# Recommender tower: the low weights' subtraction behind the gathers, the first embeddings in a quarter and a rest, and a shared relu in the first and last chunk

## What is computed

```python
e = stack([tbl_f[ids[:, f]] for f in range(39)], axis=1)   # 2048 x 39 x 16
x0 = xk = e
for W, b in layers:                                         # three layers of 128
    z = relu(einsum('bhd,bkd,hks->bsd', x0, xk, W) + b[None, :, None])
    xk, direct = z[:, :64], z[:, 64:]                       # last layer: all 128 direct
h = concat([sum_over_d(all direct parts), dense_ctx], axis=1)
y = relu(relu(h @ W_top1 + b_top1) @ W_top2 + b_top2) @ W_top3
```

## Time and profile before

| | us |
|---|---|
| median of 3 runs | 2478.97 (2478.65 to 2479.06) |
| time of the profiled execution | 2477.58 |
| its span, first to last instruction | 2475.8 |

### The profile page before, as it was taken

The page is one execution under the profiler, slowest core; times in us unless marked ns, Lnnn a source line. Parts: engine busy times, 40 slices in busy tenths (PEclk is TensorE's granted clock), DMA queues, the critical chain, the costliest instruction groups (busy, mean ns, idle before and its releaser), DMA issues.

```text
span 2475.8 us, 33269 instructions
## 1 busy us (share of the span) xinstructions
PE 2422.1 (98%) x8854; PEld 1640.9 (66%) x8854; DVE 2211.2 (89%) x1876; ACT 1724.4 (70%) x2185; POOL 1948.6 (79%) x1331
## 2 busy tenths in 40 slices
PE   5999999999999999999999999999999999999989
PEld 2566666666666666666666666666666666666655
DVE  1599999999989999999999999899999999999990
ACT  1677777777767777767777776676777777677663
POOL 6688888888878888888888888788888888865550
PEclk9899999999999999999999999999999999999999
DMA  3778667766856766776686677577668667766830
GB/s 74 157 145 175 141 138 160 158 137 141 175 124 139 174 134 140 163 157 137 144 172 138 139 161 160 121 157 160 137 139 174 145 139 154 164 136 134 171 84 0
DMA packets 214716, 352.60 MB, mean 142 GB/s; under 512 B 34382, under 2 KB 47566, under 8 KB 214588
## 3 DMA queue, kind: packets, MB, share of 16 engines
q1 hardware_dynamic: 194717, 347.07, 65.4%
q0 software_dynamic: 19968, 5.15, 2.1%
HBM read 346.97 MB, written 5.12 MB: 142 GB/s over the span
## 4 chain that ended last, share of the span: by engine, by line
PE 54%; POOL 26%; issue 14%; DVE 4%; ACT 1%; POOLq 0%; DMA 0%; ACTq 0%; DVEq 0%
PE ps L858 20%; POOL Pl L397 11%; POOL emb L391 11%; PE ps L868 11%; PE ps L848 10%; PE ps L836 8%; PE ps L831 2%; POOL dir L426 2%; DVE P L731 1%; DVE ps L731 1%; DVE Pl L736 1%; PE ps L983 1%; POOL sqx L403 1%; PE ps L975 1%; PE ps L824 1%
## 5 line engine op out<-in xcount | busy, mean ns | idle before, releaser
L397 POOL TENSOR_TENSOR Pl<-P,Ph 128x1024 fp32r<-128x1024 f32 x448 | 1074.8, 2399 | 285.3 <-ACT Ph L541 261.5
L858 PE MATMUL ps<-Ph,wh 128*128 128x512 f32 x2048 | 965.2, 471 | 9.9 <-ACT Ph L541 9.9
L541 ACT ACTIVATE Ph<-ps 128x1024 fp32r<-128x1024 f32 x576 | 590.3, 1025 | 406.7 <-DVE ps L731 393.0
L731 DVE TENSOR_TENSOR P<-xb,ps 128x1024 f32<-128x1024 f32 x704 | 853.2, 1212 | 2.8 <-DMA xb<-x_dram 2.8
L736 DVE TENSOR_TENSOR Pl<-ps,Ph 128x1024 fp32r<-128x1024 f32 x576 | 705.1, 1224 | 116.1 <-ACT Ph L541 97.4
L858 PE MATMUL ps<-Ph,wl 128*128 128x512 f32 x1920 | 755.5, 393 | 0.0
L868 PE MATMUL ps<-Pl,wh 128*128 128x512 f32 x2048 | 742.2, 443 | 7.4 <-POOL Pl L397 7.4
L391 POOL DMA_INDIRECT emb<-tbl_in,idx x624 | 600.6, 962 | 170.5 <-issue 145.0
L731 DVE TENSOR_TENSOR ps<-xb,ps 128x1024 f32<-128x1024 f32 x576 | 707.1, 1228 | 28.5 <-issue 9.4
L541 ACT ACTIVATE Ph<-P 128x1024 fp32r<-128x1024 f32 x448 | 473.9, 1058 | 186.1 <-DVE P L731 129.8
L868 PEld LDWEIGHTS ps<-Pl,wh 128*128 128x128 f32 x2048 | 384.3, 188 | 200.0 <-issue 118.2
(11 more groups left out here) (68 smaller groups left out, 857.2 us busy)
## 6 DMA issues: line engine op xcount, KB each, us to landing
xb<-x_dram SPq DMA_DIRECT2D x1280, 256.0 KB
emb<-tbl_in,idx POOLq DMA_INDIRECT x624
x_dram<-rows SPq DMA_DIRECT2D x64, 78.0 KB
xb<-w_in SPq DMA_DIRECT2D x16, 128.0 KB
xb<-wt_in SPq DMA_DIRECT2D x2, 512.0 KB, 4.4
xb<-dense_in SPq DMA_DIRECT2D x1, 768.0 KB, 5.3
wp<-w_in SPq DMA_DIRECT2D x4, 128.0 KB
xb<-w0a_in SPq DMA_DIRECT2D x1, 448.0 KB
```

Of the source, the lines that this page charges most:

```text
L397: pool.tensor_tensor(Pl[:, h_slot(ref, c, k)], P[:, p_slot(ref, c, k)], Ph[:, h_slot(ref, c, k)], ALU.subtract).then_inc(low_pool, 1)
L541: act.activation(Ph[:, h_slot(ref, c, k)], p, ACT.Copy).then_inc(rounded, 1)
L731: dve.tensor_tensor(p, xb[:, x], xk.unsqueeze(1).broadcast_to([128, 2, N]), ALU.mult)\
L858: pe.matmul(z_of(c, k), w[:, q, j, :], Ph[:, h_slot(ref, c, k), j, :], start=k in (L1B, L2) and i + j == 0, stop=False)
```

## The change

1. DVE's subtraction for `wl` and the two copies after it move from the weight preparation to behind DVE's work on the first embeddings. PE and SP wait for five weight signals at the start; PE waits for all eight only before g = 1. The staged weights move to the end of `xb`, in slots that the first spreads don't touch.
2. The first tile's embeddings are prepared in two parts: columns 0 to 3 (`D0`) first, then columns 4 to 15 (`D1`). ACT does high and full for `D0` and high for `D1`; DVE does low for `D0`, low for `D1` and full for `D1`. PE's first transposes wait for the `D0` part alone.
3. For chunk 0 ACT copies `x2` before `rows`, and PE's first two sums wait for `x2` alone.
4. In chunk 0 (first layer) and in the last chunk (second layer) DVE does the relu of the lower half in place while ACT does the direct part; ACT then copies the lower half to the upper half.
5. POOL issues 11 gathers instead of 14 ahead of the low part of k = 7, and 7 instead of 4 behind it. `WARM` is 37 instead of 36.

```diff
--- before.py
+++ after.py
@@ -34,7 +34,7 @@
 
 
 PRE = 4
-WARM = 36
+WARM = 37
 L1B, L2, STEPS = PAIRS - PRE, PAIRS, 2 * PAIRS
 KIND = "GVPVGPVGVPVGVGVGVGVP"
 SPL = [k for k in range(STEPS) if KIND[k] != "P"]
@@ -59,6 +59,7 @@
 SINGLE_STEPS = [k for k in range(STEPS) if TURN[k % PAIRS] == SINGLE // 2]
 assert all(k in SPL for k in SINGLE_STEPS)
 CHUNKS = TILES * CPT
+D0, D1 = slice(0, DC), slice(DC, D)
 NEXT_IDS_AT = (2, 0)
 GATHERS = [[1, 2, 3, 5, 9, 14, 16, 18, 19], [1, 2, 3, 5, 6, 8, 9, 10],
            [1, 2, 3, 5, 6, 9, 10, 12, 14, 16, 18, 19], [1, 2, 3, 5, 6, 8, 9, 10, 18, 19]]
@@ -185,6 +186,9 @@
         sel = sel0[0:R2, 0:T0 * R0].rearrange("p (t r) -> p t r", r=R0)
         sel0_st, inc = stage(R2, T0, R0), stage(R0, T0, NF)
         w0a_st, w0b_st = stage(R0, T0, S), stage(R0, T0, S)
+        assert at[0] + NS * 2 * S <= XSLOTS * 2 * N
+        at[0] = XSLOTS * 2 * N - NS * 2 * S
+        assert at[0] >= 2 * PRE * 2 * N
         w_st = stage(128, NS, 2 * S).rearrange("p q (j m) -> p q j m", j=2)
 
         xt = xb[:, :, :, :].rearrange("p q j n -> p (q j) n")
@@ -231,6 +235,10 @@
         emb_high = sem("emb_high")
         emb_low = sem("emb_low")
         emb_full = sem("emb_full")
+        first_high = sem("first_high")
+        first_full = sem("first_full")
+        first_low = sem("first_low")
+        first_x = sem("first_x")
         settled = sem("settled")
         aux_ready = sem("aux_ready")
         aux_read = sem("aux_read")
@@ -329,8 +337,8 @@
                         .then_inc(xb_in[q], 16)
 
 
-            sp.wait_ge(weights_made, 8)
-            sp.wait_ge(parts_made, 2)
+            sp.wait_ge(weights_made, 5)
+            sp.wait_ge(parts_made, 3)
             write_rows(0, 0)
             for p in range(PRE):
                 spread(0, p)
@@ -442,7 +450,7 @@
                 take_ids(T)
 
             next_ids(1)
-            early, early2 = 14, 18
+            early, early2 = 11, 18
             for f in range(early):
                 gather(f)
             for k in range(L1B, L2):
@@ -556,9 +564,18 @@
                 act.activation(dir1[:, COL1[c % CPT], :], z2_ps, ACT.Relu, bias=bias[:, 2:3]).then_inc(z2_read, 1)
 
 
-            high_emb(0)
-            full_emb(0)
-            copy_x(0, 0)
+            def part(x, d):
+                return x[:, :, d].rearrange("p f d -> p d f")
+
+            act.wait_ge(gathered, 16 * NF)
+            act.activation(emb_h[:, :, D0], emb[:, :, D0], ACT.Copy).then_inc(first_high, 1)
+            act.activation(emb2[:, D0, 0, :], part(emb, D0), ACT.Copy).then_inc(first_full, 1)
+            act.activation(emb_h[:, :, D1], emb[:, :, D1], ACT.Copy).then_inc(emb_high, 1)
+            act.wait_ge(aux_ready, 1)
+            act.activation(x2[:, :], aux_ps[0:R2], ACT.Copy).then_inc(first_x, 1)
+            act.activation(rows_sb, aux_ps[0:NF], ACT.Copy).then_inc(rows_ready, 1)
+            act.wait_ge(rows_ready, 1)
+            act.sem_inc(aux_read, 1)
             square(0, 2, 0, early_ps[0][1])
             rest_squares(0, 0, 1, early_ps[0][0])
             for t in range(1, FULL0):
@@ -566,9 +583,8 @@
             act.wait_ge(squares_done, 1)
             direct0(0)
             act.wait_ge(z0_read, 1)
-            upper(0, z0_ps[:, 0], xk1_upper)
             act.wait_ge(xk1_upper, 1)
-            lower(0, z0_ps[:, 0], xk1_ready)
+            act.activation(z0_ps[hi, 0], z0_ps[lo, 0], ACT.Copy).then_inc(xk1_ready, 1)
 
             act.wait_ge(rows_written, 16)
             copy_x(0, AUX)
@@ -632,9 +648,13 @@
                             direct1(c)
                         if k == RELU1_AT:
                             act.wait_ge(z1_read, T * CPT + c + 1)
-                            upper(1, z1_ps[:, c % 2], xk2_upper)
-                            act.wait_ge(xk2_upper, T * CPT + c + 1)
-                            lower(1, z1_ps[:, c % 2], xk2_ready)
+                            if end:
+                                act.wait_ge(xk2_upper, CHUNKS)
+                                act.activation(z1_ps[hi, c % 2], z1_ps[lo, c % 2], ACT.Copy).then_inc(xk2_ready, 1)
+                            else:
+                                upper(1, z1_ps[:, c % 2], xk2_upper)
+                                act.wait_ge(xk2_upper, T * CPT + c + 1)
+                                lower(1, z1_ps[:, c % 2], xk2_ready)
                         if KIND[k] != "P" and (CPT * ref + c, k) in STEPSET:
                             round_(T, ref, c, k)
                         if end and k == L1B:
@@ -698,17 +718,9 @@
             dve.wait_ge(weights_made, 1)
             dve.tensor_scalar(w0[:, :, :], w0a_st[:, 0:FULL0], 0.5, None, ALU.mult).then_inc(weights_made, 1)
             dve.tensor_scalar(w0b_st[:, FULL0], w0a_st[:, FULL0], 0.5, None, ALU.mult).then_inc(weights_made, 1)
-            dve.wait_ge(parts_made, 2)
-            dve.tensor_tensor(wl[:, :, :, :], w_st, wh[:, :, :, :], ALU.subtract).then_inc(weights_made, 1)
-
             dve.wait_ge(parts_made, 3)
             part = slice(GAP, GAP + REST)
             dve.tensor_tensor(w0x[part, :], w0b_st[part, FULL0], w0x[part, :], ALU.subtract).then_inc(weights_made, 1)
-
-            dve.wait_ge(weights_made, 5)
-            for k in SINGLE_STEPS:
-                q = SPL.index(k)
-                dve.tensor_copy(wh[K1:, q, 1, :], wl[K1:, q, 1, :]).then_inc(weights_made, 1)
 
             dve.wait_ge(incident, 1)
             dve.scalar_tensor_tensor(out=w0[0:NF, 0, :], in0=aux_ps[0:NF, 0:S], scalar=-0.5, in1=w0a_st[0:NF, 0, :],
@@ -742,9 +754,24 @@
                 dve.wait_ge(rest_square, chunk + 1)
                 dve.tensor_tensor(sqx[LOWS, :], rest_sq, sqx[LOWS, :], ALU.subtract).then_inc(rest_ready, 1)
 
+            def lower(layer, z, made):
+                dve.tensor_scalar(z, z, bias[lo, layer:layer + 1], 0.0, ALU.add, ALU.max).then_inc(made, 1)
+
+            def part(x, d):
+                return x[:, :, d].rearrange("p f d -> p d f")
+
+            dve.wait_ge(first_high, 1)
+            dve.tensor_tensor(emb2[:, D0, 1, :], part(emb, D0), part(emb_h, D0), ALU.subtract).then_inc(first_low, 1)
             dve.wait_ge(emb_high, 1)
-            dve.tensor_tensor(emb2[:, :, 1, :], emb[:, :, :].rearrange("p f d -> p d f"),
-                              emb_h[:, :, :].rearrange("p f d -> p d f"), ALU.subtract).then_inc(emb_low, 1)
+            dve.tensor_tensor(emb2[:, D1, 1, :], part(emb, D1), part(emb_h, D1), ALU.subtract).then_inc(emb_low, 1)
+            dve.tensor_copy(emb2[:, D1, 0, :], part(emb, D1)).then_inc(emb_full, 1)
+            dve.wait_ge(parts_made, 2)
+            dve.tensor_tensor(wl[:, :, :, :], w_st, wh[:, :, :, :], ALU.subtract).then_inc(weights_made, 1)
+            dve.wait_ge(weights_made, 6)
+            for k in SINGLE_STEPS:
+                q = SPL.index(k)
+                dve.tensor_copy(wh[K1:, q, 1, :], wl[K1:, q, 1, :]).then_inc(weights_made, 1)
+
             def low_weights():
                 dve.wait_ge(mlp_high, 1)
                 r = slice(2 * GAP, DX)
@@ -755,6 +782,8 @@
                         .then_inc(mlp_low, 1)
 
             rest_low(0)
+            dve.wait_ge(squares_done, 1)
+            lower(0, z0_ps[lo, 0], xk1_upper)
             dve.wait_ge(xk1_ready, 1)
             waiting = None
             for s in range(PRE):
@@ -779,6 +808,9 @@
                                 waiting = None
                             if k == L2 - 1:
                                 low_weights()
+                                dve.wait_ge(plain_done, PLAINS[CHUNKS - 1, L1B - 1])
+                                dve.wait_ge(split_done, SPLITS[CHUNKS - 1, L1B - 1])
+                                lower(1, z1_ps[lo, (CPT - 1) % 2], xk2_upper)
                             continue
                         if k == L1B:
                             dve.wait_ge(xk1_ready, T * CPT + c + 2)
@@ -897,16 +929,25 @@
                 pe.matmul(z1_ps[:, 0], wp[:, 0, 0, :], wp[:, 0:2].rearrange("p q j m -> p (q j m)"), start=True, stop=True)
 
 
-            pe.wait_ge(weights_made, 8)
+            pe.wait_ge(weights_made, 5)
             pe.wait_ge(parts_made, 1)
             pe.wait_ge(idx_ready, 2)
-            pe.wait_ge(emb_full, 1)
-            pe.wait_ge(emb_low, 1)
+            pe.wait_ge(first_full, 1)
+            pe.wait_ge(first_low, 1)
             late = None
             for g in range(2):
+                if g:
+                    pe.wait_ge(weights_made, 8)
+                    pe.wait_ge(emb_full, 1)
+                    pe.wait_ge(emb_low, 1)
                 transposes(g)
-                pe.wait_ge(aux_read, READS * g + 1)
+                if g:
+                    pe.wait_ge(aux_read, READS + 1)
+                else:
+                    pe.wait_ge(first_x, 1)
                 for i, t in enumerate((FULL0, 0, 1)):
+                    if i == 2 and not g:
+                        pe.wait_ge(aux_read, 1)
                     sums(t, early_ps[g][i])
```

## The result

The changed kernel took 2483.39 us (median of 12 runs, 2481.15 to 2485.74) beside 2479.32 us for the kernel before (12 runs): the ratio is 1.0018, with a 95% interval of 1.001 to 1.0026. It is 4 us slower, not 7 us faster. The profiled execution took 2484.04 us, its span is 2482.2.

The account below looks back on a forecast made before the run. PE, busy 98% of the span, was taken as the bound. Entering its unbroken work 6.65 us earlier plus 0.48 in the last chunk gave 7.1, so 2478.97 - 7.1 = 2471.9 us; range 2469.6 to 2475.2.

Parts of the forecast that it names:

- the first part of PE's side: Start: moving the `wl` subtraction frees a gather, 3.95 us saved; moved copies cost nothing, as PE is in warm-up matmuls.
- D: Rival, slower: clock stays at half through both groups until POOL's k = 0; 5.1 us slower, 2484.1; chance 0.04.
- The gather: POOL's early gather loses its wait for DVE's `wl` subtraction: 1.08 us instead of 5.03, saving 3.95.
- The quarter first: First embeddings: preparing a quarter first lets transposes follow the last gather after 0.84 us instead of 2.18, saving 1.34.
- `x2` first: Chunk 0: PE's first sums wait for one copy instead of two, saving 0.61 us.
- Relu: DVE's relu beside ACT's direct part: 0.71 us saved in chunk 0, 0.48 in the last chunk.
- POOL: Ids' copy held behind the moved `wl` subtraction; low part of k = 0 at 89.95 instead of 96.76, lead 6.8 us.
- The sum: PE's lead 6.6 and POOL's 6.8 let PE enter 6.65 us earlier; with the last chunk's 0.48, 7.1 us.
- The granted clock: Sign at PE in chunk 0: forecast is wrong if the clock is at half beyond 65 us or beyond 82.

Follow-up runs that it names:

- group 3: Changed kernel unchanged 2470.11 us beside 2477.86 for the kernel before, no slow stretch; with the subtraction moved back 2474.44; with 24 warm-up matmuls 2470.16.
- group 4: Changed kernel unchanged 2485.14 us, with the slow stretch; kernel before 2476.73; changed kernel with the subtraction moved back 2476.27; with 24 warm-up matmuls 2472.47.
- the first profile: Profile of the changed kernel, unchanged, from the result's own runs, with the slow stretch; that execution took 2484.04 us.
- group 2: Changed kernel unchanged 2483.65 us beside 2477.43 for the kernel before; with 36 warm-up matmuls 2482.92; with 60, 2502.1; all with the slow stretch.
- the run with the pause: Changed kernel with POOL clearing the unused buffer Pl ahead of the 14th gather: 2473.58 us, ratio 0.9988 to the kernel before.
- groups 1, 3 and 5: Changed kernel in 1: 24 warm-up matmuls 2470.79 us, 36 2470.64, subtraction back 2475.15; in 5: unchanged 2472.23, POOL pause 2473.58, early DVE work 2469.59; group 3 above.

## Why the prediction was wrong

**The step that failed** is in the first part of PE's side: that PE "is in its warm-up matmuls, whose end is 54.2 [...] and which the 37th moves to about 55.1, still before the first transposes below". I took the pace of those matmuls as given because nothing in the change touched them. They ended at 71.6 (at 55.4 in group 3, without the slow stretch), and the transposes, 14.3 us later than forecast, waited for nothing else. That this is the loss is shown by the changed kernel without the slow stretch (2470.11 in group 3) and by group 4, where 24 matmuls instead of 37 gave back 12.7 us on one chip. No rival had it: D was a loss on PE by the granted clock, which stood at its full level when the passes slowed down; that its 2484.1 lies next to the measured 2483.39 is luck. In the kernel before a delayed warm-up would have had 8.29 us of idle time in which to hide half of such a delay of 16; the change shortens that cover to about 2 us, so that what happens to unused work decides when the used work begins.

**What it costs.** The marks of the third layer in the profiles: 143.6 with the slow stretch against 132.3 in group 3's profile of the same kernel, 11.3 us, while the transposes differ by 71.47 - 57.82 = 13.7. The last 20 passes have brought the clock back, so that chunk 0's first layer runs at the full one, and at ACT's direct part the difference is 12.6 (82.31 and 69.68). At POOL's low part of k = 0 it is 11.6 (101.59 and 89.99): in group 3 that part comes 0.42 us behind POOL's own gathers, with the slow stretch POOL has long issued them and waits 2.91 us for ACT. The medians, 2483.4 and 2470.1, differ by 13.3; some 2 us of that lie in the loop, whose marks span 2274.4 us in the first profile, 2272.2 before, 2271.9 in group 3's and 2267.4 in group 2's (146.8 to 2414.2). I don't explain these.

**The other steps, by the profile of group 3 where nothing else is said.**
- The gather: 0.94 us instead of 5.03, and no wait under the small subtraction. Saved 4.1; forecast 3.95. An earlier one, at 18.6 us, took 1.83 (1.68 in the first profile) instead of 1.33. ACT's start in the first profile moved by 60.31 - 56.46 = 3.85. With the subtraction back the long gather is there again (5.02) and the kernel is slower by 4.3 us: that term is shown by removal.
- The quarter first: 56.86 to 57.82 is 0.96 us instead of 2.18, saved 1.22; forecast 1.34. DVE's piece took 0.43, not 0.34.
- `x2` first: PE's sums start 0.65 us after ACT (58.90 to 59.55) instead of 1.26, saved 0.61 as forecast.
- Relu, by the first profile: 0.63 in chunk 0 (82.31 to 83.76 instead of 75.66 to 77.74; forecast 0.71), 0.49 in the last (forecast 0.48). DVE's relu took 0.74 to 0.75, not 0.65, ACT's copy 0.57, not 0.62.
- POOL: the ids' copy was held to the end of the subtraction, 59.74 + 4.21 = 63.95, and k = 0 began at 89.99; forecast 89.95. With the subtraction back the copy took 0.21 to 0.22. The Trainium skill, SBUF — State Buffer, section "SBUF: two separate sides", has the lock last for the whole instruction, where a DVE instruction with two SBUF inputs takes it only against a GpSimd instruction that reads SBUF; the copy agrees. So does its other side: in the run with the pause, POOL's clear of a buffer reads nothing, and DVE's small subtraction with two SBUF inputs ran beside it in 0.28 us, as long as in the kernel before.
- The sum: 7.1 us forecast. The terms as measured on PE's side give 4.1 + 1.22 + 0.61 + 0.63 + 0.49 = 7.05, POOL's lead at k = 0 was 96.76 - 89.99 = 6.8, and the medians in group 3 differ by 7.7 (2477.86 - 2470.11). With the subtraction back 2.7 and 3.4 us remain, which with the gather's 4.1 make 6.8 and 7.5. The granted clock was back at 1.00 by 65 us and, after a second stretch at half, by 82, as hoped.

**What stays open.** What the slow stretch is: PE's issue is held for some 16 to 21 us, and some of its completion signals are late; the hold ends at 60.6 to 61.0 whatever PE has left to do. Shown is that it came with the moved subtraction in the result's own group and in groups 2 and 4 (in the records of 36, 37 and 60 warm-up matmuls; with 24 only as the late completion), that it did not come in groups 1, 3 and 5, and that in group 4, on one chip, the slow passes came neither in the kernel before nor with the subtraction moved back. Whether the missing pause in the gathers or DVE's idleness at 23 to 27 us brings it wasn't told apart. That a signal of PE was late at 22 to 25 us in three profiles of groups 2 and 4, and by 0.8 us in the version with the subtraction back, leaves it possible that something of the kind is at work on such a chip whatever the kernel, and that the moved subtraction only makes it visible or worse; no run tests this. That the slow stretch ends 1.7 to 2.1 us after DVE's second subtraction has begun (59.03 to 60.96 in the first profile) may be chance: counted from the start of the span the ends agree as closely. It is also open whether the kernel before would show it with another warm-up, and why one group has it and another not: each had a chip of its own, so that the chip and the occasion aren't told apart.

## What to carry to other kernels

Work that only fills time is still ahead of the real work in its engine's queue: when a change brings the real work forward, cut the filler with it (here 24 matmuls lose nothing where 37 do no harm, 2470.16 beside 2470.11 us, and save 2485.14 - 2472.47 = 12.7 us where they do, the first of these from one execution) rather than leave 2 us between them. Price a change with the cover that remains after it, for every engine, not with the cover that it had. And when two versions that should be equal differ by far more than their scatter, run both on the same chip before explaining it: here an innocent constant looked like 13 us, and the ratio of the same kernel to the same other one was 0.9968 in one group and 1.0024 in another.

## What was not expected of the hardware

In some groups, each on its own chip, PE issued one weight load or one pass only every 1.4 us for 16 to 21 us, at a granted clock of 1.00 at first, while the other engines kept their pace: POOL's gathers took 0.94 to 0.95 us during it, and ACT's and DVE's first pieces of the embeddings 0.33 and 0.43 to 0.44 us, in group 3 0.33 and 0.43. By their times all executions of the changed kernel in such a group were affected alike (12 of 2481.15 to 2485.74 us, where the undisturbed ones took 2470), and those of the kernel before, timed beside them, were not (2476.69 to 2482.58). Signals of PE's completion could be late too, by 0.8 to 2.5 us, even while its passes followed each other without a gap (DVE's correction at 24.92 in group 4's control).
